# Spreading the last batch's residual work of three FFNs over the next layer's first ten score units, and loading the expert weights later

## The reference

```python
x = x + tanh(g_xattn[l]) * xattn_l(layernorm(x), ctx, ctx, ...)
x = x + tanh(g_ffn[l])   * ffn_l(layernorm(x), ...)
```

## Time and profile before

| | |
|---|---|
| median of 3 runs | 832.74 us (832.41 to 835.34) |
| the profiled execution's own time | 834.32 us |
| its span, first to last instruction | 832.5 us |
| mean granted TensorE clock | 0.844 of full speed |
| PE busy | 638.8 us, 77% |
| DVE busy | 543.0 us, 65% |
| ACT busy | 326.1 us, 39% |
| POOL busy | 261.4 us, 31% |

### The profile page before, as it was taken

The page is one execution under the profiler, slowest core; times in us unless marked ns, Lnnn a source line. Parts: engine busy times, 40 slices in busy tenths (PEclk is TensorE's granted clock), DMA queues, the critical chain, the costliest instruction groups (busy, mean ns, idle before and its releaser), DMA issues. The chain is left out here.

```text
span 832.5 us, 9949 instructions
## 1 busy us (share of the span) xinstructions
PE 638.8 (77%) x2926; PEld 397.5 (48%) x2926; DVE 543.0 (65%) x1451; ACT 326.1 (39%) x627; POOL 261.4 (31%) x470
## 2 busy tenths in 40 slices
PE   5788775566779998884888870348887898989997
PEld 3433333354665564552534330124343576767875
DVE  8775635888772553485736655863558798878655
ACT  3044552233224344353143440214544455545554
POOL 4343365111011312113250721001122445445463
PEclk9577987688869999896599985555998899999999
DMA  8864311002204323006044320222500232333341
GB/s 253 187 177 132 73 37 46 2 0 64 63 12 140 90 41 91 1 1 182 9 123 156 57 76 0 62 64 67 169 6 2 63 103 93 103 113 106 112 121 57
DMA packets 67989, 67.71 MB, mean 81 GB/s; under 512 B 25119, under 2 KB 48223, under 8 KB 67552
## 3 DMA queue, kind: packets, MB, share of 16 engines
q1 hardware_dynamic: 61326, 64.61, 28.4%
q10 hardware_dynamic: 6610, 2.47, 1.2%
HBM read 50.29 MB, written 17.60 MB: 82 GB/s over the span
## 5 line engine op out<-in xcount | busy, mean ns | idle before, releaser
L783 ACT ACTIVATE PT<-ps 110x512 f32<-110x512 f32 x192 | 110.5, 595 | 137.3 <-PE ps L1645 63.4
L1217 DVE TENSOR_REDUCE mraw<-ps 128x4 f32<-128x308 f32 x256 | 116.0, 476 | 73.6 <-PE ps L1605 23.7
L1605 PE MATMUL ps<-KG,QG 98*128 98x308 f32 x256 | 113.0, 477 | 49.4 <-DVE mraw L1217 34.1
L693 POOL TENSOR_TENSOR sg<-sg,cb 128x512 f32<-128x512 f32 x64 | 83.8, 1312 | 78.3 <-ACT sg L945 74.9
L1605 PEld LDWEIGHTS ps<-KG,QG 98*128 98x128 f32 x256 | 59.2, 237 | 94.4 <-DVE mraw L1217 70.4
L1645 PE MATMUL ps<-QG,KG 128*110 128x512 f32 x192 | 93.1, 506 | 9.1 <-ACT PT L783 6.7
L1461 DVE TENSOR_TENSOR ps<-ps,sg 128x512 f32<-128x512 f32 x72 | 50.3, 698 | 39.3 <-POOL sg L693 36.3
L1665 PE MATMUL ps<-PT,VN 128*18 128x512 f32 x512 | 73.0, 644 | 0.0
L525 POOL CAST mhl<-mraw 128x64 fp32r<-128x64 f32 x16 | 5.0, 310 | 192.7 <-DVE mraw L1217 180.0
L945 ACT ACTIVATE sg<-ps 128x512 f32<-128x512 f32 x72 | 43.0, 597 | 46.4 <-PE ps L1864 45.7
L1645 PEld LDWEIGHTS ps<-QG,KG 128*110 128x110 f32 x192 | 35.0, 187 | 54.4 <-ACT PT L783 38.8
(11 more groups left out here) (284 smaller groups left out, 1414.9 us busy)
## 6 DMA issues: line engine op xcount, KB each, us to landing
cb<-c_parts SPq DMA_DIRECT2D x64, 256.0 KB, 3.3
QG<-q_parts SPq DMA_DIRECT2D x48, 256.0 KB, 3.9
KG<-k_parts SPq DMA_DIRECT2D x48, 154.0 KB, 3.0
q_parts<-hiT SPq DMA_DIRECT2D x14, 256.0 KB, 2.0
q_parts<-loT SPq DMA_DIRECT2D x14, 256.0 KB, 2.3
k_parts<-kmH SPq DMA_DIRECT2D x16, 154.0 KB, 2.4
k_parts<-kmL SPq DMA_DIRECT2D x16, 154.0 KB, 2.6
VN<-v_parts SPq DMA_DIRECT2D x16, 144.0 KB, 2.9
```

Of the source, the lines that this page charges most:

```text
L693: pool.tensor_tensor(sg[:, n % 3, :], sg[:, n % 3, :], cb[:, k % CRING, :], ALU.mult).then_inc(sc_done, 1)
L783: act.activation(PT[0:w, q % PTR, :], ps[0:w, 4 + q % 2, :], ACT.Exp, scale=SCALE[l]).then_inc(exp_done, 1)
L1217: dve.tensor_reduce(mraw[:, n % 2, i, g * HG:(g + 1) * HG], ps[:, u % 2, 0:GK].rearrange("p (h k) -> p h k", k=K), AX_X, ALU.max).then_inc ...
L1605: ins = pe.matmul(o, QG[0:KS, n % 3, g, q], KG[0:KS, n % 3, g, :], start=True, stop=l not in (1, 2))
```

## The change

Three moves, and two entries of a list:

- The calls of `residual(3)` at the end of `ffn0`, `ffn1` and `ffn2` are gone. Their instructions are cut into parts, and in pass k = -1 of the next attention one part follows each `maximum` of batch 1: `last_of_ffn0(u)`, `last_of_ffn1(u)`, `last_of_ffn2(u)` for unit u = 0 to 9. The instructions are the same.
- ACT's `normalise_out` of batch 3 moves from pass k = -1 to pass k = 0, both at c = 8, between `weigh(0, 8)` and `weigh(0, 9)`.
- SP's wait for `f1_ps` and the loads of the gate weights and of `low` move from the head of layer 2 to behind the loads of batch 8's maxima.
- (4, 1) and (5, 1) leave `OWN`: their Newton steps and shifts go from DVE to POOL.

```diff
-        OWN = [(0, 0), (0, 1), (4, 0), (5, 0), (4, 1), (5, 1)] + [(2, b) for b in range(B)] + [(7, b) for b in range(B)]
+        OWN = [(0, 0), (0, 1), (4, 0), (5, 0)] + [(2, b) for b in range(B)] + [(7, b) for b in range(B)]
...
             for l in range(L):
-                if l == 2:
-                    sp.wait_ge(f1_ps, B)
-                    sp.dma_start(mst[:, :, :], a["moe_gate"]).then_inc(ld_moe, 16)
-                    sp.dma_start(low[:, :, :], a["low"].partition_broadcast(P)).then_inc(ld_moe, 16)
                 for k in range(-2, B):
...
+                    if l == 2 and k == -1:
+                        sp.wait_ge(f1_ps, B)
+                        sp.dma_start(mst[:, :, :], a["moe_gate"]).then_inc(ld_moe, 16)
+                        sp.dma_start(low[:, :, :], a["low"].partition_broadcast(P)).then_inc(ld_moe, 16)
...
-                        if c == 8 and k == -1 and l >= 1:
+                        if c == 8 and k == 0 and l >= 1:
                             normalise_out((2 * l + (l > 1), 3))
...
+            def last_statistics(src, p):
+                tiles = range((B - 1) * TPB, B * TPB)
+                s = slice((B - 1) * TPB, B * TPB)
+                if p < 2:
+                    for i in tiles[2 * p:2 * p + 2]:
+                        ins = dve.bn_stats(st[:, i, :], src[:, i, :])
+                    if p == 1:
+                        link(ins)
+                if p == 2:
+                    for i in tiles:
+                        ins = dve.bn_aggr(mv[:, i, :], st[:, i, :])
+                    link(ins)
+                if p == 3:
+                    dve.tensor_scalar(nhv[:, s], mv[:, s, 1], EPS, -0.5, ALU.add, ALU.mult)
+                    link(dve.tensor_scalar(var[:, s], mv[:, s, 1], EPS, None, ALU.add))
+                    dve.tensor_scalar(rs[:, s].bitcast(I32), var[:, s].bitcast(I32), -0.5, RSQRT_GUESS,
+                                      ALU.mult, ALU.add).then_inc(stats_ready, 1)
+
+            def last_root(m, p):
+                s = slice((B - 1) * TPB, B * TPB)
+                v, t, y = nhv[:, s], nt[:, s], rs[:, s]
+                if p == 0:
+                    dve.wait_ge(stats_ready, LN_ORDER.index(m) + 1)
+                if p < 3:
+                    link(dve.tensor_tensor(t, v, y, ALU.mult))
+                    link(dve.tensor_tensor(t, t, y, ALU.mult))
+                    link(dve.scalar_tensor_tensor(out=y, in0=t, scalar=1.5, in1=y, op0=ALU.add, op1=ALU.mult))
+                if p == 3:
+                    link(dve.tensor_tensor(nsh[:, s], mv[:, s, 0], rs[:, s], ALU.mult))
+                    dve.tensor_scalar(nsh[:, s], nsh[:, s], -1.0, None, ALU.mult).then_inc(own_shift, 1)
+
+            def last_of_ffn0(u):
+                xs = x[:, (B - 1) * TPB:B * TPB, :]
+                if u == 0:
+                    dve.wait_ge(f0_ps, B)
+                    dve.scalar_tensor_tensor(out=xs, in0=ps[:, 6 + (B - 1) % 2, :].rearrange("p (t d) -> p t d", d=D),
+                                             scalar=tg[:, 4:5], in1=xs, op0=ALU.mult, op1=ALU.add).then_inc(f0_done, 1)
+                    dve.wait_ge(f0_done, B)
+                if 1 <= u <= 4:
+                    last_statistics(x, u - 1)
+                if 5 <= u <= 8:
+                    last_root((2, B - 1), u - 5)
...
                     for c in range(NCH):
                         for b, u in units_of(l, k, c):
                             maximum(b, u // G, u % G)
+                            if l >= 1 and k == -1:
+                                (last_of_ffn0, last_of_ffn1, last_of_ffn2)[l - 1](u)
...
-                residual(3)
```

More of the change, by code:

```diff
@@ new lines, in last_of_ffn1 @@
+            def last_of_ffn1(u):
+                s = slice((B - 1) * TPB, B * TPB)
+                if u == 0:
+                    dve.wait_ge(inner_ready, B)
+                    link(dve.tensor_tensor(xn[:, s, :], xn[:, s, :], rows[:, R_GAM, :].unsqueeze(1).to_broadcast([P, TPB, D]), ALU.mult))
+                if u == 1:
+                    link(dve.tensor_tensor(xn[:, s, :], xn[:, s, :], rows[:, R_BET, :].unsqueeze(1).to_broadcast([P, TPB, D]), ALU.add))
+                if u == 2:
+                    link(dve.scalar_tensor_tensor(out=x[:, s, :], in0=xn[:, s, :], scalar=tg[:, 5:6], in1=x[:, s, :], op0=ALU.mult, op1=ALU.add))
+                if 3 <= u <= 6:
+                    last_statistics(x, u - 3)
@@ new lines, in last_of_ffn2 @@
+            def last_of_ffn2(u):
+                xs = x[:, (B - 1) * TPB:B * TPB, :]
+                if u == 0:
+                    dve.wait_ge(f2_ps, B)
+                    dve.scalar_tensor_tensor(out=y8[:, :, :], in0=ps[:, 6 + (B - 1) % 2, :].rearrange("p (t d) -> p t d", d=D), scalar=am[:, 6:7],
+                                             in1=rows[:, R_FB2, :].unsqueeze(1).to_broadcast([P, TPB, D]), op0=ALU.mult, op1=ALU.add).then_inc(f2_read, 1)
+                    dve.wait_ge(f2_read, B)
+                if u == 1:
+                    link(dve.scalar_tensor_tensor(out=xs, in0=y8[:, :, :], scalar=tg[:, 6:7], in1=xs, op0=ALU.mult, op1=ALU.add))
+                if 2 <= u <= 5:
+                    last_statistics(x, u - 2)
+                if 6 <= u <= 9:
+                    last_root((7, B - 1), u - 6)
```

## The result

| | changed kernel | kernel before, same chip |
|---|---|---|
| median | 845.48 us (839.72 to 846.16, 4 runs) | 834.04 us (832.41 to 843.65, 4 runs) |
| ratio, 95% interval | 1.0126 [1.0086, 1.0166] | |
| profiled execution | 839.72 us, span 837.9 us | 834.32 us, span 832.5 us |
| mean granted TensorE clock | 0.846 | 0.844 |

It is slower, by 1.3%. A second set of runs gave 843.01 and 1.0109 [1.0062, 1.0156]. The forecast, +7.3 us or 1.0088, lies in both intervals, and 840.0 is 5.5 us under the first median. The ratios leave out runs that lie over 1.5% above the fastest of their kernel, which takes out 12 of 35 runs of the kernel before in one set and 2 of 23 and 2 of 17 in the others, so where a ratio and the plain medians of all runs disagree I give both: here +10.5 and +11.4 us in the first set, +9.1 and +6.3 in the second.

What follows compares the result with a forecast made beforehand. No engine is full; a chain through all of them at three joints bounds the kernel. Layer 1 -0.4, layer 2 +2.8, layer 3 +4.9 give +7.3 on the median 832.74: 840.0 us, range 834.5 to 846.0.

Steps and rivals of the forecast that it cites:

- The bound of each joint: Into each layer: residual(3) holds DVE in 1; late queries, then POOL's chain in 2; residual hidden in 3.
- Interleaving, layer 1: Into layer 1: PE may start unit 10 2.3 us sooner, with 0.4 us charged for a clock that rises later.
- First maximum of layer 2: Into layer 2: the first maximum comes at 386.2 in place of 391.17, a gain of 5.0 us (bounds 3.6 and 6.6).
- the queries' 6.6: Into layer 2: gain with the gate weights moved and none of the delay from (4, 1), the upper bound.
- the 1.6 of delay by (4, 1): Layer 1's FFN: with (4, 1) refined on POOL, ACT's inner_out(1) is 1.6 us later, delaying inner_sum(3) on DVE.
- POOL's chain late: Into layer 2: statistics end later, so the split for PE's turn of batch 9's maxima is 4.8 us late.
- Behind the stop: Layer 2, behind PE's 5.9 us stand: 1.7 us for the moved normalisation plus 1.3 for the low clock.
- Layer 3: Into layer 3: residual(3) now comes behind the first maximum, so unit 10's maximum is 3.2 us later; nothing saved.
- The normalisation: Pass k = 0: ACT delays PE's chunk 11, costing 1.5 us in layer 1, 1.7 each in layers 2 and 3.
- ACT has the slack: Rival: moved normalisations cost nothing and the clock stays up, leaving +0.7 us, 833.4 us; chance 0.14.
- The second payment isn't fixed: Rival: POOL's 6.99 and 6.74 us gaps aren't tied to following an all-reduce and vanish; 826.1 us; chance 0.05.
- Nothing overlaps: Rival: contention and low clock in layer 1, slow POOL refinements, 0.48 us maxima; some +12 us, 844.7 us; chance 0.26.

Runs made afterwards that it cites:

- sp_only: Only the gate-weight load moved behind batch 8's maxima loads, against the kernel before: 828.18 us, ratio 0.9928.
- after_order: Changed kernel with POOL's all-reduce of the 8-bit weight's maximum put ahead of the refinement and shift of (5, 3) in layer 2: 834.66 us, ratio 0.9983 to the kernel before.
- after_warm: Changed kernel plus a 128x1 POOL tensor_tensor on unused columns directly behind layer 2's all-reduce of am: 836.18 us, ratio 0.9992 to the kernel before.
- after_normback: Changed kernel with batch 3's normalise_out back in pass k = -1 at c = 8: 839.62 us, ratio 1.0031 to the kernel before.
- interleave_only: Only the three FFNs' last residuals spread over the next layer's units, against the kernel before: 843.79 us, ratio 1.0055.
- own_only: Only the Newton steps and shifts of (4, 1) and (5, 1) moved from DVE to POOL, against the kernel before: 838.91 us, ratio 1.0058.
- norm_only: Only ACT's normalisation of batch 3 moved from pass -1 to pass 0, against the kernel before: 843.71 us, ratio 1.0111.

## Why the prediction was right, and where its sizes were off

**The bound of each joint** was named rightly: PE's 7.63 us, POOL's chain behind it, the residual hidden in layer 3. `sp_only`, `after_order` and `after_warm` show them one by one by taking them away. The signs named for the profile after are there: DVE idle for 2.19 and 8.70 us before unit 0 in layers 1 and 3, PE's 6.03 us for `mhl`, and waits of 1.07, 0.82 and 1.53 us for the exponential, where about 1.6 was said.

**Interleaving, layer 1**: -2.3, measured -2.18. The joint 4-5 is -2.19 as well, so the +0.4 for the clock behind unit 10 did not come. In the eight traces with the spreading this joint is -2.05 to -3.12. (the earlier trace rows show only pairs of maxima; the 0.48 us of a single one stand in the rows of DVE above.)

**First maximum of layer 2**: -5.0, measured -4.0 (391.17 to 386.81 is -4.36, and the FFN's second turned input came 0.41 sooner). The -7.16 of the joint 7-8 holds besides 2.4 that this execution gained at the FFN's start, where no edit is, and 0.75 of the next paragraph. Counted the same way the five traces with these edits give -4.0 twice, -2.4 in `after_order` and `after_warm`, and -5.1 in `after_normback`. In all of them PE stops 2.74 to 2.76 us for ACT. The clock is at 0.50 behind it for 3.4 us in the first two, for 6.8 in the next two, and not at all in the last. So the queries' 6.6 (`sp_only` measured 6.75) and the 1.6 of delay by (4, 1) were right. The term that the sum left out is the clock behind this stop, 0 to 2.7 us; it charged the clock only behind the stop of 6 us.

**POOL's chain late**: +4.8, measured 4.77 from the first maximum to the turn (39.57 us from 386.81 to 426.38, for 34.80 from 391.17 to 425.97). The joint 8-9 shows +5.53 because its first mark comes 0.75 sooner: the split of batch 8's maxima no longer collides with DVE's residual. POOL's chain hangs on the statistics and gains nothing by that.

**Behind the stop**: 1.7 + 1.3 = 3.0, measured 2.17 and 2.15, of which PE's wait for the exponential is 0.82. But the same stretch is +2.43 in `after_normback` and +3.45 in `interleave_only`, which don't have the normalisation there, and +4.50 in `after_warm`, which has it. Behind the turn the clock is at 0.50 for 3.4 us in the changed kernel, 6.0 in `after_normback`, 5.0 and later 3.5 more in `interleave_only`, and 9.5 in `after_warm`. So the two terms can't be read apart, and how near 3.0 came is in part luck.

**Layer 3**: +3.2, measured 3.01 at unit 10. By the next mark +0.96 is left of it; against `sp_only` and `own_only`, whose 12-13 is -2.04, it is 3.0.

**The normalisation**: 1.5, 1.7, 1.7; the joints give 1.3, 1.5, and PE's wait of 1.53 in layer 3. For the sum of 4.9 the kernels say 2.0 to 9.3, by the way of counting. Behind 13 in layer 3, where most of the excess of `norm_only` sits, kernels without any edit also differ by 2 to 7 us. What decides the clock there stays open.

**The sum.** By the joints: layer 1 -0.9, layer 2 -4.0 + 4.8 + 2.2 = +3.0, layer 3 +3.9 (12 to 14); +6.0 for the +7.3 predicted. The ratios say +9.1 [5.2, 13.0] and +10.5 [7.2, 13.8]. The parts alone, -6.0, +9.3, +4.8 and +4.6, add up to +12.7 by the ratios, each with some 3 or 4 us of interval; by the plain medians they are -8.5, +7.0, +1.7 and +7.1, +7.3 in all, and the second set of the whole is +6.3. So the order of size and the mechanism are shown. The ratios leave 3 to 4.5 us that no row explains, and the medians of the larger set leave none: both profiled executions of the changed kernel are the fastest of their set, and the slower ones have no trace. That the time came so near +7.3 is in part luck: in these traces the clock gives or takes 1 to 3 us at each of several places, with the same edits.

**The rivals.** "ACT has the slack" is refuted by the waits of 0.82 to 1.53 us for the exponentials. "The second payment isn't fixed" is refuted by `after_warm`: it is fixed to the first tensor_tensor behind an all-reduce. Of the first payment the Trainium skill (GPSIMD Engine Reference, Instruction dispatch) says some 6 us that no instruction shows; the idle times in front of the all-reduces in all traces here, 5.57 to 6.25 us, agree. "Nothing overlaps" had the wrong places (contention in layer 1 did not come), though its 844.7 is nearer to both medians; as a difference its +12 is nearer than +7.3 to the first set's +10.5 and not to the second's +9.1.

## What to carry to other kernels

Before work is spread to fill an engine's idle time, ask what it is hidden under now and who waits for its last result: the same spreading gained 2.2 us where the residual was exposed, lost 3 where another engine's gap hid it, and lost 5 where a longer chain hung on its statistics. Read a small effect between marks and in several executions, since one profile can be 2 to 4 us off at a joint without an edit. When an instruction is put behind a slow one, follow its result to the engine that waits for it, and see what is queued behind that wait; here the new order on POOL took a stop of 6 us away where the normalisation stood a pass later, and made one of 5.62 us where it did not. Price a delay in front of TensorE at more than its length when it makes a stop longer: here 1.6 us of delay cost another 0 to 2.7 us through the clock.

## What the runs showed of the hardware

- The second idle time on POOL, put down to issue, stands before the first TENSOR_TENSOR behind a PARTITION_ALL_REDUCE in all kernels whatever its size: 6.67 to 7.18 us (128x308), 6.63 to 7.51 (128x64), 7.66 to 7.95 (128x4), 6.79 to 7.55 (128x1), in 28 cases of 14 traces. A CAST between them is not held: in layer 3 it runs at 556.93, and the 7.11 us come behind it.
- Behind a stop of TensorE of 2.74 to 2.76 us, with the clock at 1.00 up to it, the granted clock went to 0.50 in five traces (for 3.4 us in `own_only` and the changed kernel's two, for 6.8 in `after_order` and `after_warm`) and stayed at 1.00 in the sixth, `after_normback`. Behind the stop of 1.17 us at the same place it stayed at 1.00 in all eight others.
- The kernel before, with no change of program, spread from 826.88 to 847.07 us in 35 runs. Traces place part of such a spread: at 12-13 and 13-14 by the clock, and at the start by a load of queries that PE waited for, 4.37 us (at 63.19) in one execution of the changed kernel and 2.04 (at 60.08) in the other.
